# Routed experts moved into a phase of their own, over gathered rows, in a two-layer decoder kernel

## What is computed

```python
x = ln(x + attn0(x))               # 16 heads of 16, causal, bias from cos/sin of distance
x = ln(x + cross0(x, ctx))         # 64 context rows
x = ln(x + moe(x))                 # 8 routed experts (best 2 of 8 per token) + 2 shared
x = ln(x + attn1(x))               # causal, low-rank projections
x = ln(x + cross1(x, ctx))
x = ln(x + ffn1(x))                # 256 -> 1024 -> 256

def moe(x):                        # x: 8192 tokens x 256
    logits = x @ router_w + router_b
    gates = softmax(top 2 of logits, the rest -inf)
    expert = lambda w1, w3, w2: silu(x @ w1) * (x @ w3) @ w2     # 256 -> 128 -> 256
    return sum_e gates[:, e] * expert(routed e) + sum_s expert(shared s)
```

## Time and profile before

| what | us |
|---|---|
| median of 3 runs | 3673.79 (3671.61 to 3683.06) |
| the profiled execution | 3679.51 |
| its span | 3677.7 |
| mean granted TensorE clock, share of full | 0.958 |
| phase 1, from 64 us to the last store's issue | to 1341.3 |
| phase 2, from there to the last store's issue | to 3037.2 |

### The profile page before, as it was taken

The page is one execution under the profiler, slowest core; times in us unless marked ns, Lnnn a source line. Parts: engine busy times, 40 slices in busy tenths (PEclk is TensorE's granted clock), DMA queues, the critical chain, the costliest instruction groups (busy, mean ns, idle before and its releaser), DMA issues.

```text
span 3677.7 us, 60188 instructions
## 1 busy us (share of the span) xinstructions
PE 3361.8 (91%) x20814; PEld 2507.0 (68%) x20814; DVE 2627.9 (71%) x7168; ACT 2228.8 (61%) x4067; POOL 1009.4 (27%) x1560
## 2 busy tenths in 40 slices
PE   2999999999999838999999999999999874899998
PEld 1777777777777625677777777777777653666665
DVE  5588888888888744667777776777777633688876
ACT  3577767776777632355555555555555543577776
POOL 1144434443444431222222222222222210000000
PEclk8999999999999968999999999999999966899999
DMA  6554446544554221445444444444444412011010
GB/s 188 90 92 88 82 86 106 95 77 84 100 107 70 32 86 34 78 77 92 87 87 91 93 87 92 90 87 93 93 89 80 79 27 80 12 35 34 25 35 23
DMA packets 203405, 283.31 MB, mean 77 GB/s; under 512 B 48929, under 2 KB 131874, under 8 KB 194274
## 3 DMA queue, kind: packets, MB, share of 16 engines
q1 hardware_dynamic: 203106, 279.46, 38.9%
HBM read 179.49 MB, written 96.73 MB: 75 GB/s over the span
## 4 chain that ended last, share of the span: by engine, by line
PE 77%; DMA 6%; DVE 6%; ACT 4%; issue 3%; POOL 2%; SPq 1%; POOLq 0%; ACTq 0%; DVEq 0%
PE ps L816 36%; PE ps L969 10%; PE ps L943 9%; PE ps L983 7%; PE ps L1167 5%; DMA k_stack<-qk_scratch 5%; PE ps L918 2%; PE ps L947 2%; PE ps L1043 2%; ACT pt L1645 1%; POOL pt L1845 1%; PE ps L994 1%; PE ps L957 1%; SPq L1970 1%; PE ps L1053 1%
## 5 line engine op out<-in xcount | busy, mean ns | idle before, releaser
L1645 ACT ACTIVATE pt<-ps 128x512 f32<-128x512 f32 x1280 | 724.1, 597 | 275.4 <-PE ps L969 229.5
L1845 POOL TENSOR_SCALAR_AFFINE_SELECT pt<-pt 128x256 f32<-128x256 f32 x1024 | 390.4, 419 | 905.8 <-ACT pt L1645 905.8
L943 PE MATMUL ps<-k_stack,q_stack 96*128 96x512 f32 (+3 forms) x2048 | 590.8, 348 | 49.8 <-DMA k_stack<-qk_scratch 34.4
L1324 DVE CUSTOM_DVE_ANT_0 ps<-ps,future 128x512 f32<-128x512 f32 (+3 forms) x1024 | 481.7, 514 | 107.5 <-PE ps L943 101.4
L969 PE MATMUL ps<-q_stack,k_stack 100*128 100x512 f32 (+3 forms) x2048 | 534.5, 344 | 15.3 <-ACT pt L1645 10.3
L943 PEld LDWEIGHTS ps<-k_stack,q_stack 96*128 96x128 f32 x2048 | 387.5, 195 | 135.3 <-DMA k_stack<-qk_scratch 40.0
L1317 DVE TENSOR_REDUCE nmax<-ps 128x1 f32<-128x512 f32 (+2 forms) x768 | 359.3, 504 | 118.6 <-PE ps L947 115.5
L969 PEld LDWEIGHTS ps<-q_stack,k_stack 100*128 100x128 f32 x2048 | 346.8, 193 | 87.4 <-ACT pt L1645 34.6
L1851 POOL TENSOR_TENSOR rs<-rs,mhalf 128x4 f32<-128x4 f32 x96 | 97.1, 1012 | 1061.8 <-DVE rs L1360 1060.4
L983 PE MATMUL ps<-pt,v_ones 128*32 128x512 f32 (+3 forms) x4096 | 313.1, 448 | 14.6 <-POOL pt L1845 14.6
L1629 ACT ACTIVATE q_stack<-ps 4x512 fp32r<-4x512 f32 x512 | 261.4, 574 | 52.5 <-PE ps L957 50.0
(11 more groups left out here) (274 smaller groups left out, 7846.7 us busy)
## 6 DMA issues: line engine op xcount, KB each, us to landing
qk_scratch<-parts SPq DMA_DIRECT2D x64, 1024.0 KB, 6.2
q_stack<-qk_scratch SPq DMA_DIRECT2D x384, 128.0 KB, 6.3
k_stack<-qk_scratch SPq DMA_DIRECT2D x384, 128.0 KB, 6.8
gate_of<-gate_scratch SPq DMA_DIRECT2D x128, 256.0 KB, 6.3
x_mid<-x_ring SPq DMA_DIRECT2D x32, 512.0 KB, 4.1
x_ring<-x_mid SPq DMA_DIRECT2D x32, 512.0 KB, 4.7
x_ring<-in_x SPq DMA_DIRECT2D x16, 512.0 KB, 3.9
out_dram<-x_ring SPq DMA_DIRECT2D x16, 512.0 KB, 2.9
```

Source lines behind the costliest of these rows:

```text
L943: done = e.matmul(bank(bank_of[piece])[:, at:at + width], a.q[0:96, base + h, t * P:(t + 1) * P], a.k[0:96, base + h, 0:width], start=True ...
L1324: done = e.tensor_tensor_reduce(src, src, future[:, SEQ - width:SEQ], -1.0, 3e38, ALU.add, ALU.min, nmax[:, g % 2, u // 5 * 2 + h, t:t + 1])
L1645: e.activation(dst, src, ACT.Exp).then_inc(exp_up.sem)
L1845: done = e.affine_select(out=blk, in_=blk, compare_op=ALU.is_ge, fill=0.0, base=0, pattern=[[0, 2], [1, P]], channel_multiplier=-1)
```

## The change

A phase 4 is put between phases 1 and 2 (`PHASES = (1, 4, 2, 3)`), with a barrier more.

**Phase 1** now ends each batch with the router: rt transposes the normed rows (8 transposes, ACT copies, no low part), gr is 8 fp32 matmuls, gt and ge some 36 small DVE operations (best two, gates, running count per expert), rk 8 bf16 matmuls that give each token its rank among those of its expert. sx writes each token's number into `token_of`, at its expert's list and rank, by 8 indirect DMAs on POOL's queue (2 for each of 4 tiles of 128 tokens). The attention's output projection (tm p0) becomes 8 whole fp32 matmuls of 256 columns in place of 24 in fp32r. The mask matmul reads a small `diag` tile. The prologue also zeroes token_of.

**Phase 4's prologue** turns the counts into a list of 39 tiles of 512 rows (32 for all of 2 × 8192 rows, 7 for the rounding up of eight experts), on DVE, loads the token numbers by an indirect DMA, and now holds the low-rank weight product and the loads of phase 2's weights, 2 chunks in place of 9. Then each **tile** gathers its expert's weights (one indirect DMA of 384 KB) and 512 rows of x_mid[0] (four of 128 KB), and computes one expert on them.

**Phase 2** keeps the two shared experts, whose second product is now a tm (24 matmuls of 256 columns, tag sh). yg gathers each token's two routed rows from sorted_y (8 indirect DMAs of 128 KB), two batches ahead, and cb adds them with their gates (8 DVE operations of 128x256). Router, gate stores and loads, POOL's gate multiply, dn and bk are gone.

The table is new for every phase but 3: periods 81.62, 74.38 and 31.45, and for phase 4:

```diff
+PHASES = (1, 4, 2, 3)
+COUNT = {1: BATCH, 2: BATCH, 3: BATCH, 4: TILES}
...
 TABLE = {
-    1: (71.3, {
+    1: (81.62, {
...
-    2: (91.43, {
+    2: (74.38, {
...
+    4: (6.4, {
+        "tensor": {
+            "mt": [-6],
+            "mu": [-3, -1.5],
+            "md": [3.6],
+        },
+        "scalar": {
+            "mw": [-8],
+            "mt": [-5.2],
+            "m1": [0],
+            "m3": [2],
+            "my": [5.4],
+        },
+        "vector": {
+            "mw": [-7],
+            "mt": [-4.6],
+            "m1": [0.6],
+            "m2": [1.3],
+            "m3": [2.6],
+        },
+        "gpsimd": {
+            "mg": [-16],
+        },
+        "sync": {
+            "ms": [6.6],
+        },
+    }),
...
+    if ph == 4:
+        put("mg", b)
+        put("mw", b)
+        put("mt", b)
+        put("mu", b, 0)
+        put("mu", b, 1)
+        for kind in ("m1", "m2", "m3", "md", "my", "ms"):
+            put(kind, b)
...
+        put("tc", "rt", b)
+        for kind in ("gr", "gt", "rk", "ge"):
+            put(kind, b)
+        for t in range(TT):
+            put("sx", b, t)
     elif ph == 2:
         put("tc", "ex", b)
-        for kind in ("gr", "gt", "ge", "gg", "gh"):
-            put(kind, b)
-        for i in range(ALL):
+        put("yg", b)
+        put("cb", b)
+        for i in range(SHARED):
...
-            for c in range(CT):
-                put("dn", b, i, c)
-        for r in range(EXPERTS):
-            put("sg", b, r)
-        put("bk", 2, b)
+        put("tm", "sh", b)
...
+        rows_banks, up_banks, down_banks = Banks([0, 1]), Banks([2, 3, 4, 5]), Banks([6, 7])
+        for piece in turns[4]["tensor"]:
+            take({"mt": rows_banks, "mu": up_banks, "md": down_banks}[piece[0]], piece, 4, 1 if piece[0] == "mu" else 2)
+        score_banks, turned_banks, other = Banks([0, 1]), Banks([2, 3]), Banks([4, 5, 6, 7])
...
+                elif kind == "mu":
+                    i, which = key
+                    k = i % 2
+                    e.wait_ge(*mw_lo[i,])
+                    e.wait_ge(*mt_lo[i,])
...
+                    product(e, bank(bank_of[piece]), ops).then_inc(mu_up.sem)
+                elif kind == "md":
+                    i, = key
+                    k = i % 2
+                    e.wait_ge(*m3_lo[key])
...
+                elif kind == "sx":
+                    b, t = key
+                    e.wait_ge(*ge_up[b,])
+                    for k in range(2):
+                        to = bass.IndirectOffsetOnAxis(ap=place_i[:, b * TT + t, k:k + 1], axis=0)
+                        e.indirect_dma_start(token_of[:, :], to, id_c[:, b * TT + t:b * TT + t + 1], None).then_inc(
+                            id_spread[b % RING].sem, 16)
+                elif kind == "mg":
+                    i, = key
+                    if i >= 2:
+                        e.wait_ge(*mw_lo[i - 2,])
+                    of = bass.IndirectOffsetOnAxis(ap=w_rows_i[:, i:i + 1], axis=0)
+                    e.indirect_dma_start(mw_st[:, i % 2, :], None, dram["w_routed"], of).then_inc(mw_in[i % 2].sem, 16)
+                    if i >= 3:
+                        e.wait_ge(*mt_up[i - 3,])
+                    for t in range(TT):
+                        of = bass.IndirectOffsetOnAxis(ap=rows_i[:, t, i:i + 1], axis=0)
+                        e.indirect_dma_start(mx_st[:, i % 3, t, :], None,
+                                             x_mid[0].rearrange("b p t d -> (b p t) d"), of).then_inc(mx_in[i % 3].sem, 16)
+                elif kind == "yg":
+                    b, = key
+                    if b >= 2:
+                        e.wait_ge(*cb_up[b - 2,])
+                    for t in range(TT):
+                        for k in range(2):
+                            of = bass.IndirectOffsetOnAxis(ap=place_i[:, b * TT + t, k:k + 1], axis=0)
+                            e.indirect_dma_start(y_st[:, b % 2, k, t, :], None, sorted_y[:, :], of).then_inc(
+                                y_in[b % 2].sem, 16)
...
+                elif kind == "ms":
+                    i, = key
+                    e.wait_ge(*my_up[key])
+                    e.dma_start(sorted_y[i * SEQ:(i + 1) * SEQ, :].rearrange("(t p) d -> p t d", p=P),
+                                my[:, i % 2, :, :]).then_inc(ms_out[i % 2].sem, 16)
```

More of the change, by code:

```diff
@@ L78, with __init__ @@
 class Signal:
-    def __init__(self, sem, keys, per, step):
+    def __init__(self, sem, keys, per, step, start=0):
         self.sem, self.per, self.step = sem, per, step
-        self.at = {key: (n + 1) * per * step for n, key in enumerate(keys)}
+        self.at = {key: start + (n + 1) * per * step for n, key in enumerate(keys)}
+        self.end = start + len(keys) * per * step
     def __getitem__(self, key):
@@ L436, in times_of @@
     out = {engine: {} for engine in ENGINES}
-    for b in range(BATCH):
+    for b in range(COUNT[ph]):
         place = {}
@@ new lines, in decoder @@
+        mw_in = [signal(f"mw_in{k}", "gpsimd", "mg", 1, 16, lambda key, k=k: key[0] % 2 == k, (id_spread[3], None)[k])
+                 for k in range(2)]
+        y_in = [signal(f"y_in{k}", "gpsimd", "yg", 2 * TT, 16, lambda key, k=k: key[0] % 2 == k, mx_in[k])
+                for k in range(2)]
+        ms_out = [signal(f"ms_out{k}", "sync", "ms", 1, 16, lambda key, k=k: key[0] % 2 == k) for k in range(2)]
+        mw_hi, mw_lo = signal("mw_hi", "scalar", "mw", then=xe_exp), signal("mw_lo", "vector", "mw", then=xs_max)
@@ new lines, in decoder @@
+        mt_up, mt_hi, mt_lo = (signal(n, e, "mt", CT, then=was) for n, e, was in
+                               (("mt_up", "tensor", xv_up), ("mt_hi", "scalar", xq_hi), ("mt_lo", "vector", xq_lo)))
+        mu_up, md_up = signal("mu_up", "tensor", "mu", then=xq_up), signal("md_up", "tensor", "md", then=xs_up)
+        m1_tanh, m1_up = signal("m1_tanh", "scalar", "m1", then=xp_copy), signal("m1_up", "vector", "m1", then=xs_add)
+        m2_up = signal("m2_up", "vector", "m2", then=vx_up)
+        m3_hi, m3_lo = signal("m3_hi", "scalar", "m3", then=xo_hi), signal("m3_lo", "vector", "m3", then=xo_lo)
@@ L529, in decoder @@
+        my_up = signal("my_up", "scalar", "my", then=ge_exp)
+        cb_up = signal("cb_up", "vector", "cb")
         up_up = signal("up_up", "tensor", "up")
@@ L877, in tensor @@
                         product(e, bank(q), ops).then_inc(kt_up)
-                elif kind == "prologue" and key[0] == 2:
+                elif kind == "prologue" and key[0] == 4:
                     e.wait_ge(low_parts, 2)
@@ L1818, in gpsimd @@
                     done.then_inc(consts.sem)
-                    e.wait_ge(consts.sem, KM_READY + 2)
-                elif kind == "prologue":
+                    e.wait_ge(consts.sem, KM_READY + 4)
+                    e.wait_ge(block_up, 1)
+                    of = bass.IndirectOffsetOnAxis(ap=block_i[:, 0:1], axis=0)
+                    blocks = token_of.rearrange("(b s) one -> b (s one)", s=SEQ)
+                    e.indirect_dma_start(id_list[:, :], None, blocks, of).then_inc(list_in, 16)
+                    e.wait_ge(list_in, 16)
+                elif kind == "prologue" and key[0] == 3:
                     e.memset(ones[:, :], 1.0)
@@ L1899, in sync @@
                         e.dma_start(ff_c[:, :], dram["ff_c"]).then_inc(ff_in3, 16)
-                    first = chunks[ph][0][3]
+                    first = chunks[ph][0][3] if chunks[ph] else 0
                     for w, at, cols, n in chunks[ph]:
@@ L1913, in sync @@
                     if ph == 1:
+                        e.wait_ge(zero_up, 1)
+                        whole = token_of.rearrange("(p s) one -> p (s one)", p=P)
+                        for k in range(TT):
+                            e.dma_start(whole[:, k * P:(k + 1) * P],
+                                        place_i[:, :, :].rearrange("p n k -> p (n k)")).then_inc(zero_home, 16)
                         e.wait_ge(ctx_parts, 2)
@@ L1926, in sync @@
                         e.wait_ge(ctx_home, 32)
-                    elif ph == 2:
-                        e.wait_ge(small_in, 112)
-                    else:
+                        e.wait_ge(zero_home, 16 * TT)
+                    elif ph == 4:
+                        e.wait_ge(small_in, 176)
+                    elif ph == 3:
                         e.wait_ge(down_in, 16)
-                if kind == "end":
+                if kind == "end" and key[0] == 4:
+                    for k in range(2):
+                        i = TILES - 2 + k
+                        e.wait_ge(*ms_out[i % 2][i,])
+                elif kind == "end":
                     for k in range(RING):
                         e.wait_ge(*x_out[k][key[0], BATCH - RING + k])
+                        if key[0] == 1:
+                            e.wait_ge(*id_spread[k][BATCH - RING + k, TT - 1])
                 if kind in ("prologue", "end"):
```

629 lines of the change are left out of this document (421 added, 208 removed), and 235 rows, old and new, of the table TABLE.

## The result

The changed kernel took 3986.88 us (median of 4 runs, 3979.51 to 3997.77) where the kernel before took 3677.59 beside it: a ratio of 1.0844, interval 1.0811 to 1.0876. It is slower, as the likeliest case had it, but by 309 us where +71 was forecast, and outside the range. The profiled spans differ by 3977.8 − 3677.7 = 300.1 us, and I account for that.

A forecast was written before the change was run, and what follows sets the result against it. PE was taken to bound phases 1 and 2. From 3679.5 us, 54 + 18 + 0 + 422 − 322 − 101 = +71 gave 3750.5, less 5.7 = 3745 us; range 3600 to 3890, the forecast's own 3690 to 3800.

The forecast's parts named there:

- the likeliest case: Whole kernel: the prediction's own case, slower by 0.3 to 3%, at 3745 us; chance 0.35.
- Phase 1's pace: Phase 1, steady batches: 75.5 us a batch, +3.6 over 15 intervals, +54 us in all.
- PE's work: Phase 1, PE per batch: cheaper projection against new transposes, router and rank matmuls, net +1.3 us.
- The scatters: Phase 1, POOL: eight indirect scatter issues add 8 us a batch, to 31.5, and stay under PE's 72.6.
- The walk: Phase 1: following the new order group by group, PE stands idle 2 to 3 us more a batch.
- the floor is 73.2: Phase 1: no engine passes PE's 72.6 us, so a batch takes at least 73.2; the +20 us end.
- The walk's 8.6: Phase 4: one tile in written order takes 8.6 us at full clock, bound by latency; 10.0 taken between clocks.
- Rival (c): Phase 4: gathers run one after another, or the clock stays low; tiles of 12.2 us, +86, 3831 us; chance 0.13.
- Phase 2's pace: Phase 2, steady batches: attention chain bounds, PE no longer; 92.5 falls to 71 us a batch, −322 us in all.
- The forecast's stretch without experts: Phase 2 before the change: four groups of attention and projections after the last expert took 72 us, supporting 71.
- Fill and tail: Phase 2's start and end: fill of 129 us falls to about 65, tail loses 37; −101 us together.
- Rival (b): Phases 1 and 2 run at their written periods, 81.62 and 74.38 us: +143, 3888 us; chance 0.15.

The follow-up runs named there:

- e9: e8 with a third buffer of routed weights, so a gather waits for the split three tiles back; 3728.14 us, ratio 1.0125.
- e6: The changed kernel without phase 1's 128 scatters of token numbers; 3869.73 us (a single run), phase 1 at 80.1 us a batch.
- e8: e5 plus scatters at four idle places of POOL, token rows gathered ahead of weights, and 8 filler matmuls a batch in phase 2; 3803.09 us, ratio 1.0343.
- e3: The changed kernel with phase 4's tanh ahead of the next tile's weight split on ACT and DVE; 3938.12 us, ratio 1.0706.
- e5: The changed kernel with a third set of q and k rows in phase 2 and phase 4's mt straight behind the first mu; 3889.63 us, ratio 1.0587.
- e12: e11 with a fifth slot of x in phase 2 and its load 25 us earlier in SP's order; 3776.23 us, ratio 1.0258.
- e10: e9 without phase 2's gathers of routed results from the third batch on; 3718.07 us (a single run).
- e11: e9 without the 8 filler matmuls a batch in phase 2; 3726.04 us, ratio 1.0117.
- e7: The changed kernel without phase 1's router (transposes, logits, gates, ranks, scatters); 3936.79 us (a single run), phase 1 at 80.2 us a batch.

## Why the prediction was wrong

**What bounds the kernel now: right; the paces were misread.** I took 71.9 and 92.5 us for a batch. The first is the width that I had given the windows: any window of a stretch that PE fills shows PE full, so it proves nothing about the pace. The pace was 74.5. The second, from the first and last eh, mixes the short first intervals with the steady 96.4. In the differences most of this cancels, but it made the written periods (71.3 and 91.43) look kept within 1.2%, when each steady phase in fact runs 4.5 to 5.4% over its own: 71.3 → 74.5, 91.43 → 96.4, and after the change 81.62 → 85.5 and 74.38 → 78.4.

**Phase 1's pace, the step that failed: 75.5 forecast, 85.5 steady, +195 instead of +54.** Of its three terms two were wrong: PE's new work was put at 1.3 us and is 4.1, and the eight scatters were put at no cost and took 5.4. With the walk's 1.4 they make 74.5 + 10.9 = 85.4.
- *PE's work*, "net +1.3": it is +4.1 in e9's window. By the distances of starts there (672.5 to 992.5, a batch), the router's product has 1.8, its transposes 0.6, the ranks at least 0.2, and about 1 is that the old products (S and T above all) follow each other more slowly; why isn't shown. The last part is the projection, "from 24 matmuls at 0.117 to 8 at 0.23 (1.9)". The 128 matmuls written in the kernel are 256 records in the trace, and the router's 128 are 256 too; the groups of PE after:

```profile
L903 PE MATMUL ps<-w_out,oh 128*128 128x256 f32 x256 | 58.8, 383 | 0.8 <-ACT oh L1890 0.8
...
L903 PE MATMUL ps<-router_w,xT 128*128 128x8 f32 x256 | 33.6, 267 | 0.7 <-ACT xT L1890 0.7
```

 Successive records of the first start 0.21 us apart, so a plain fp32 matmul of 256 columns costs 0.42, and the eight 3.3 us, more than the 2.8 that they replace. I had read the four records of the earlier trace rows in 1.88 us as four matmuls; they are two.
- *The scatters*, "POOL gets 8 issues, +8, no engine passes PE's": the size was right (0.98 busy and 0.3 behind it), the conclusion wrong. POOL at 41 of 86 us is far from full, and yet the eight issues cost 5.4 us a batch (e6) until they stood where POOL was idle (e8). The share of busy time didn't show this; the place in the written order did.
- *The walk*, "PE idle 2 to 3 us more": right in size, and on the safe side. PE stands 2.0 us a batch in e6 and e9 where it stood 0.6; the 5.6 to 6 of the changed kernel are this and the scatters.

The upper end that I gave, the written period, 81.62 and +146, was itself passed. "No engine passes PE's 72.6, so the floor is 73.2" was a floor for an order that nobody had made.

**Phase 4: right.** 9.70 us a tile against 10.0, clock .85 and POOL near 50%, as the text wanted; +401 against +422. The walk's 8.6 at the full clock holds as well: between tiles that fell wholly in full clock the starts lie 8.5 to 9.3 us apart. The mechanism too: latency in the written order, since e3, e5 and e8 took the tile to 8.4, 8.5 and 8.1 by order alone, and e9 to 6.7 with a buffer more (with the doubt that e12 leaves). The wait named for it, the two token splits between m2 and the next mu, is the one that ends last; what the walk missed is that the tanh ahead of them stood behind the next tile's weights. The issue of a gather costs POOL 0.95 plus 0.30, not 1.01.

```profile
L2180 POOL DMA_INDIRECT mx_st<-x_mid,rows_i x147 | 139.2, 947 | 44.8 <-issue 44.8
```

Rival (c), gathers one after another, fell: in e9 five of them fit in 6.73 us. The view of DMA issues of e9 (1600 to 1800; count, median us from issue to landing) has 

```profile
mx_st<-x_mid,rows_i POOLq DMA_INDIRECT x111, 3.7
```

The Trainium skill's page "DMA: Bandwidth & Descriptors", section "Anatomy of one DMA — SWDGE (gpsimd) path", gives 2.0 us plus bytes over 436 GB/s for one transfer, by which 128 KB would take 2.3. No run here has one alone; beside the others it is 3.7, and five of them did not add up to the 12.1 us that the prediction worked out from it.

**Phase 2's pace: right in kind, 71 forecast, 78.4 steady.** PE stands 8 us of a batch, so it no longer fills it. Missed were the rows of k, 3.3 us a batch (e5). PE's work was too low as well, 53 for about 62: the sum began at 92.5 with 90.4 of PE, where a true batch has 94.3, and here too S and T follow each other more slowly than before. Of the rest, 75.1, POOL's gathers (e10) and the ring of x (e12) have about 1 us each. The clock isn't excluded: no run took the stretches at 1.2 GHz away (10 us a batch or more remain even with the filler of e8), filler costs PE's time itself, and in e10 batches with more low clock were longer. Beside it a loop through PE, DVE, ACT and POOL in the written order is left, with many waits of 0.2 to 1.6 us. Which of them closes it stays open. The forecast's stretch without experts was a drain and had no next batch's loads, layer norms and projections in it. **Fill and tail**, −101 against −59: the tail got 12 us longer (133.7 to 146.1), where I had taken 37 off.

**The rivals.** Rival (b), the written periods, gave 3888 at a chance of 0.15 and was the nearest: its fault was to have the periods kept exactly. At the paces that were in fact run, 85.5 and 78.4, its own sum gives (10.0 + 7.4) × 15 = 261 over the forecast, 4006, 19 above what was measured; the other errors (the end of phase 1, the fill and tail, phase 4, and a pace before of 94.6 and not 92.5 in phase 2) nearly cancel, which is luck. So the paces were the cause, and the written periods were the best sign of them. The chance of slower, 0.63, was on the right side. What the text named as proof of an error, "phase 1 above 78", is what happened.

**Is there a version that beats both?** Not among these. e11 took back 261 of 309 us and stands 1.2% above the kernel before. Its phase 1 alone stands at (1399.5 − 185.8) − (1286.8 − 184.1) = +111 us against before, over twice the 48 still missing; with PE at 78 of 80 us there, over half of it is PE's 4.1 us a batch.

## What to carry to other kernels

Take a pace from the recurrence of one instruction, never from windows of a width you chose; then compare it with what the schedule was written for, because a hand-written order ran 4.5 to 5.4% over its own period in all four steady stretches. Price a new instruction by the place in its queue as well as by its duration: the same eight issues cost 5.4 us in one place and about 1 in another on an engine half idle. When work is removed, look for what it had covered: here a row load with two buffers. And read the clock of a batch beside its pace before comparing two runs: e7's 80.2 and e6's 80.1 are equal only by it.

## What was not expected of the hardware

- A plain fp32 matmul stands as two records (128 written, 256 recorded), with starts 0.21 us apart at 256 columns: 0.42 us each, against 3 × 0.117 = 0.35 for the three fp32r matmuls that give the same product.
- An indirect DMA occupies POOL for 0.95 us and 0.30 more before the next, for 512 bytes of token numbers, 128 KB of rows or 384 KB of weights alike (means 0.98, 0.95, 0.95). The one load of the token lists took 1.99.
- A lower clock costs a batch what PE's slack doesn't take up. In phase 2 of e11 two batches at .86 and .91 took 75.6 and 75.3 us; in e10 one at .89 had 3.0 us more of PE's time than one at .95, and none of it was taken up; in phase 1 of e7 batches at .94 took 4.0 us more than those at 1.00.
- The same instructions of phase 4 ran at 6.8 and 8.0 us a tile in e11 and e12, with only the buffers' places in memory and the chip changed. No run tells why.
